# A memset on GpSimd between consecutive indirect DMAs, in a linear-attention and mixture-of-experts kernel

## What is computed

```python
q, k, v, gate = x @ Wq.T, x @ Wk.T, x @ Wv.T, x @ Wg.T     # 16 heads of 8
beta  = sigmoid(x @ Wb.T)
alpha = exp(-exp(A_log) * softplus(x @ Wa.T + dt_bias))
for t in range(512):                                        # the delta rule
    S = S * alpha_t
    delta = (v_t - k_t @ S) * beta_t
    S = S + outer(k_t, delta)
    y_t = q_t @ S
x = layernorm(x + (rmsnorm(y) * norm_w * silu(gate)) @ Wo.T + bo)
e = argmax(x @ router_w.T)                                  # one of 8 experts per token
ye = (silu(x @ gate_w[e].T) * (x @ up_w[e].T)) @ down_w[e].T    # inner size 352
out = layernorm(x + ye)
```

## Time and profile before

| | us |
|---|---|
| median of 3 runs | 781.5 |
| lowest, highest | 775.88, 783.81 |
| profiled execution, its own time | 779.52 |
| span of its profile | 777.7 |
| TensorE busy | 677.5 |
| VectorE busy | 610.1 |
| GpSimd busy | 654.0 |
| ScalarE busy | 415.8 |

### The profile page before, as it was taken

The page is one execution under the profiler, slowest core; times in us unless marked ns, Lnnn a source line. Parts: engine busy times, 40 slices in busy tenths (PEclk is TensorE's granted clock), DMA queues, the critical chain, the costliest instruction groups (busy, mean ns, idle before and its releaser), DMA issues.

```text
span 777.7 us, 13705 instructions
## 1 busy us (share of the span) xinstructions
PE 677.5 (87%) x3545; PEld 507.4 (65%) x3545; DVE 610.1 (78%) x1554; ACT 415.8 (53%) x1281; POOL 654.0 (84%) x800
## 2 busy tenths in 40 slices
PE   8779798989989899999989989697788879999990
PEld 3446374756657575565756657575667879999990
DVE  3899999999999999999999999999953523333340
ACT  6735456564565656466565555433314346666660
POOL 2899899999999999999999999999755756766664
PEclk9889899999999999999999999799869999999995
DMA  6733233443333334333234232206346456777720
GB/s 175 198 97 98 69 98 86 114 116 90 86 90 94 89 112 116 96 85 102 82 105 120 77 97 71 85 22 220 136 164 184 166 182 226 240 237 235 238 97 9
DMA packets 135917, 97.27 MB, mean 125 GB/s; under 512 B 95630, under 2 KB 110225, under 8 KB 135714
## 3 DMA queue, kind: packets, MB, share of 16 engines
q1 hardware_dynamic: 130514, 87.55, 38.2%
q0 software_dynamic: 4320, 8.43, 3.4%
q10 hardware_dynamic: 1008, 0.43, 0.2%
HBM read 39.80 MB, written 31.43 MB: 92 GB/s over the span
## 4 chain that ended last, share of the span: by engine, by line
DVE 35%; PE 29%; POOL 20%; issue 5%; ACT 5%; DMA 3%; SPq 2%; POOLq 0%; DVEq 0%; ACTq 0%
PE banks L432 11%; DVE banks L1817 6%; DVE upd L1805 6%; POOL q_prod L1255 6%; PE banks L654 5%; PE banks L445 5%; DVE banks L1791 5%; DVE prod L1775 4%; DVE banks L1801 4%; DVE mix L1795 3%; POOL u L1255 3%; DVE upd L1786 3%; POOL solve L1255 2%; POOL kkqk L1255 2%; POOL u_tmp L1255 1%
## 5 line engine op out<-in xcount | busy, mean ns | idle before, releaser
L1255 POOL TENSOR_TENSOR q_prod<-s_keep,q_gam 128x512 f32<-128x512 f32 x128 | 139.9, 1097 | 12.0 <-ACT s_keep L965 11.7
L707 PE MATMUL banks<-q_prod,ident 128*128 128x256 f32 x496 | 118.9, 395 | 21.6 <-POOL q_prod L1255 21.4
L965 ACT ACTIVATE s_keep<-banks 128x128 f32<-128x128 f32 x128 | 49.8, 389 | 156.7 <-DVE upd L1805 156.6
L707 PEld LDWEIGHTS banks<-q_prod,ident 128*128 128x128 f32 x496 | 95.7, 198 | 46.2 <-POOL q_prod L1255 32.4
L542 DVE TENSOR_TENSOR hid<-banks,silu 128x384 f32<-128x384 f32 x71 | 39.6, 557 | 96.4 <-PE banks L432 83.8
L432 PE MATMUL banks<-xs_t,w_tile 128*128 128x128 f32 x852 | 108.9, 278 | 3.5 <-ACT silu L473 3.5
L1817 DVE TENSOR_REDUCE banks<-upd 128x128 f32<-128x640 f32 x127 | 105.0, 827 | 7.6 <-ACT z_s L1194 0.5
L432 PEld LDWEIGHTS banks<-xs_t,w_tile 128*128 128x128 f32 x852 | 102.4, 194 | 4.4 <-issue 4.3
L1791 DVE TENSOR_REDUCE banks<-prod 128x64 f32<-128x576 f32 x128 | 93.7, 732 | 0.0
L654 PE MATMUL banks<-kkqk,ident 128*128 128x320 f32 (+2 forms) x272 | 84.5, 471 | 7.7 <-ACT y_rms L993 4.3
L1775 DVE TENSOR_TENSOR prod<-banks,k_gam 128x512 f32<-128x512 f32 x128 | 88.1, 688 | 2.9
(11 more groups left out here) (214 smaller groups left out, 1442.3 us busy)
## 6 DMA issues: line engine op xcount, KB each, us to landing
w_tile<-gate_up_we SPq DMA_DIRECT2D x71, 352.0 KB, 3.0
xs<-x_sorted SPq DMA_DIRECT2D x71, 64.5 KB, 2.4
x_ct<-in_x_ct SPq DMA_DIRECT2D x16, 256.0 KB, 3.2
k_dram<-kq_s SPq DMA_DIRECT2D x16, 256.0 KB, 2.9
q_dram<-kq_s SPq DMA_DIRECT2D x16, 256.0 KB, 3.6
out<-v_s SPq DMA_DIRECT2D x16, 256.0 KB, 2.7
out<-beta SPq DMA_DIRECT2D x16, 256.0 KB, 2.6
k_h<-k_dram SPq DMA_DIRECT2D x16, 256.0 KB, 3.0
```

Source lines behind the costliest of these rows:

```text
L707: i = mm(out, ident[:, :], q_prod[m][:, :, d, :], start=(m == 0 and d == 0), stop=(d == DH - 1), skip_group_check=True)
L1255: b.step(label, win, lambda: tt(out, x, y, op))
```

## The change

GpSimd gets a buffer `pause` of 128x128 float32, which nothing reads, and a semaphore `s_pause`. In `to_sorted`, from group 24 on, it clears `pause` after each indirect DMA, and each next indirect DMA waits for that. In `scatter` it does the same after the tiles 0 to 66 of 71. The 40 memsets of `to_sorted` and the 67 of `scatter` count on one semaphore. Nothing is taken away. The buffer is allocated ahead of those of the expert stage that follow, which lie 512 bytes further on in each partition.

```diff
+        pause, s_pause = sb("pause", [P, 128]), sem("s_pause")
...
         def to_sorted(eng, t0, t1):

             for m in range(t0, t1):
+                if m > WA * TW:
+                    eng.wait_ge(s_pause, m - WA * TW)
                 eng.indirect_dma_start(t["x_sorted"], bass.IndirectOffsetOnAxis(ap=place[:, m:m + 1], axis=0),
                                        x1_all[:, m, :], None).then_inc(s_sorted_a if m < WA * TW else s_sorted, 16)
+                if m >= WA * TW:
+                    if m > WA * TW:
+                        eng.wait_ge(s_pause, m - WA * TW)
+                    nc.gpsimd.memset(pause[:, :], 0.0).then_inc(s_pause, 1)
...
             def scatter(tile):
                 after(eng, s_norm, tile)
+                eng.wait_ge(s_pause, NT - WA * TW + min(tile, NF - 4))
                 eng.indirect_dma_start(t["out"],
                                        bass.IndirectOffsetOnAxis(ap=xs[tile % NR][:, D:D + 1].bitcast(I32), axis=0),
                                        rows_out[tile % NO][:, :], None, bounds_check=past_end, oob_is_err=False) \
                     .then_inc(s_scat[tile % NO], 16)
+                if tile < NF - 4:
+                    nc.gpsimd.memset(pause[:, :], 0.0).then_inc(s_pause, 1)
```

## The result

The changed kernel takes 796.76 us (median of four runs, 795.28 to 797.96) against 781.23 of the kernel before (four runs beside it, 775.88 to 783.81): a ratio of 1.0207, 95% interval 1.0150 to 1.0264. It is about 2% slower; the interval reaches from 1.5% to 2.6%. The forecast was 783.1 within 776 to 788, no change. The medians are 15.5 us apart. The two profiled executions lie further apart: 797.96 us with a span of 796.2, which is 18.5 more than the span of 777.7 before.

What follows compares the result with a forecast made beforehand. Bounds: SyncE's weight loads at the changeover, TensorE in the expert stage, GpSimd alone at the end. Sort-out 0.2, ScalarE 0, expert stage 0, end 1.4 sum to 1.6 us; on the median 781.5 that gives 783.1, range 776 to 788.

Steps and rivals of the forecast that it cites:

- The memset, 0.20 us: Each added 128x128 memset on GpSimd: 0.20 us, by a straight line between traced 128x1 and 128x2048 memsets.
- The lower price of 0.11 us: GpSimd's memset if only its length counted: 0.11 us, making the six at the end 0.6 us cheaper.
- G: Cost of a pause between two indirect DMAs: their new distance less 1.26 us.
- G in the sort-out, 0.20: Pause between to_sorted's DMAs: 0.20 us taken, so 23 pauses make the last DMA 4.6 us later.
- G for the scatters, 0.23: Pause between scatter DMAs: 0.23 us taken, within 0.18 to 0.29; a memset ahead of an rstd adds 0.22.
- The slack of 4.4 us: Changeover to the second part: last sort-out DMA lands 4.4 us before SyncE's weight loads finish, leaving 0.2 us exposed.
- Expert stage, 0: 640 to 752 us: GpSimd falls behind 3.2 us in rounds of four scatters, hidden, caught up later; cost 0.
- The cover of 3.7 us: Expert stage: rstd ended at 683.85, its reader rows_out started at 687.55, so 3.7 us of GpSimd's backlog is hidden.
- The end, 1.4: After the rstd of 752.89: four pauses between scatters and two memsets before an rstd add 1.4 us, bounds 0.4 to 1.7.
- the pause is dear: Rival: memset costs 0.46 us, G 0.40 to 0.51, sort-out and end expose 10.3 us, giving 791.8; chance 0.10.
- The last test that the prediction named: Expert stage: the forecast is wrong if xs_t waits for ScalarE's rows_out in the rounds of four.
- its second test: Changeover to the second part: the forecast is wrong if TensorE restarts over 2 us later.

Runs made afterwards that it cites:

- e1: The changed kernel with all memsets, the waits for them moved from the indirect DMAs to the next memset: 781.41 us against 782.01 before, ratio 0.9983.
- e2: The changed kernel with the two waits ahead of a DMA swapped, the memset's written first: 782.26 us against 782.01 before, ratio 0.9992.
- e5: The kernel before with the change in scatter alone, none in to_sorted: 796.43 us, ratio 1.0183 against before.
- f7: The kernel before with 128x720 memsets in scatter only and no DMA waiting for them: 797.47 us against 781.37, ratio 1.0200.
- f3: The kernel before, without memsets, each scatter given a second wait (s_var) that is always met already: 780.46 us against 781.37, ratio 0.9999.
- f6: The changed kernel with memsets of 128x1 instead of 128x128, all waits kept: 787.88 us against 781.37 before, ratio 1.0077.
- e4: The kernel before with the change in to_sorted alone, scatters as before: 783.03 us, ratio 1.0014 against before.
- f0: The changed kernel once more, word for word: 798.15 us against 781.37 before, ratio 1.0219.
- g9: The kernel before with two weight loads instead of five ahead of SyncE's wait for x_sorted, plus to_sorted's pauses; slower chip: 799.14 us against 818.88, ratio 0.9765.
- k4: The kernel before with the change in to_sorted alone, on a slower chip: 805.62 us against 821.11, ratio 0.9841.
- k0: The changed kernel again, on a slower chip: 802.71 us against 821.11 before, ratio 0.9800.
- k1: The changed kernel with all memsets but no DMA waiting for one, on a slower chip: 819.58 us against 821.11 before, ratio 1.0001.
- e6: The changed kernel with memsets of 128x1, all waits kept, on a slower chip: 808.54 us against 821.73 before, ratio 0.9863.
- e3: The kernel before, without memsets, each scatter given a second, always met wait (s_var), on a slower chip: 822.52 us against 821.73, ratio 1.0014.
- k5: The kernel before with the change in scatter alone, on a slower chip: 817.46 us against 821.11, ratio 0.9965.

## Why the prediction was wrong, by its own steps

- **The memset, 0.20 us: right**, 0.22 to 0.23. The Trainium skill (Perfetto Trace Analysis, GPSIMD Engine Instruction) advises against taking GpSimd's reported spans at face value. Here they add up: 0.96 + 0.22 + 0.28 = 1.46, the measured distance. The lower price of 0.11 us, which the prediction itself inferred beside that rule, did not come.
- **G in the sort-out, 0.20: right for a DMA with one wait**, 1.46 - 1.26. The prediction's seams were the measured ones: 0.17 without a wait (e1) and 0.28 with the own semaphore, a difference of 0.11, its very allowance from the earlier trace rows. It missed the second size. Five of the DMAs of the last block are the first of a call and wait for `place` too, 0.50 more each. From the first to the last DMA of the block it is 636.79 - 600.60 = 36.19 us, before 627.68 - 598.55 = 29.13: 7.1 more = 23 x 0.20 + 5 x 0.50.
- **G for the scatters, 0.23: the step that failed.** It is 0.70 (1.98 - 1.28). The prediction bounded it at 0.29 by rows in which a wait for GpSimd's own result comes alone, and wrote that a wait for the memset is added without counting what the scatter waits for already. `scatter` has `after(eng, s_norm, tile)` on the line above. e2 against the change shows that the order of the two waits alone, in `scatter` and in `to_sorted`, is worth 14.5 us, 796.76 against 782.26. Nearly all of it is the scatters' (e5, 796.43).
- **The slack of 4.4 us: right.** The last DMA landed 3.07 us after its start, as the earlier trace rows had it. From the `rstd` of window 15 to TensorE's restart it is 40.58 to 41.19 us where the sort-out is that of before (before, e5, f7, f3), 41.00 with the last block 2.0 us longer (e1), 40.83 and 41.58 with 4.5 (f6, e2), and 42.19, 42.68 and 43.10 with 7.1 (e4, the change, f0). SyncE's weight loads come last at the changeover in e1 and e2; in f6, e4, the change and f0 it is the landing of the last DMA. So the edge lies near 4.5 us. Of 7.1 us 2.7 would be exposed; measured are 1.6 to 2.5, in part because the `xs` load took 1.93 us instead of 2.38 in the change. Predicted were 0.2, for 4.6 us: the slack held, and the five second waits were missing.
- **Expert stage, 0: wrong by the failed term and by nothing else.** The formula of the step stands: with G = 0.70 a round of four gets 3 x 0.70 + 0.22 = 2.32 more, 0.38 were to spare, so six rounds fall behind by 11.6; measured 11.3. The cover of 3.7 us stands too, and ScalarE's idle time behind it took up a further 1.9. (The prediction's 0.96 us of idle time per tile is too high: by the earlier trace rows it is (112.00 - 73.99) / 52.8 tiles = 0.72. Nothing else hangs on it.) But the prediction's rounds of three had 1.67 - 0.68 = 1.0 us to catch up with. Now 2 x 0.70 + 0.22 = 1.62 of the 1.67 are gone (6.25 against 6.36 us), the backlog is carried through eleven rounds to the end, and from 7.5 us on TensorE waits for it.
- **The end, 1.4: the count right, the price not.** With G = 0.70 four pauses and two memsets are 4 x 0.70 + 2 x 0.22 = 3.2; measured 3.2. In e1, at 0.09, it was 15.14 - 14.48 = 0.7.
- **The rival "the pause is dear"** pointed the right way and not at the cause. It named 791.8 us and more, put the edge at G = 0.42, said that the rounds of four run away beyond it, and had 10% of the chance. It looked for the price in the memset's length, 0.46 us; the price is in the wait, and with a memset of 0.13 us the seam is 0.78 still (f6).
- **The last test that the prediction named** was the right one: DMAs over 1.6 us apart and `xs_t` late in the rounds of four. TensorE's restart over 2 us later, its second test, came too (4.2, of which 2.1 are the sort-out). In the changed profile the first hole of TensorE is ahead of a matmul of gate and up:

```profile
684.56 1.60 PE L439 MATMUL banks<-xs_t,w_tile 128*128 128x128 f32 x12 [1.61 <-ACT xs_t L469]
```

None of the experiments on chips of the first kind beats the kernel before: e1 and e2 equal it. On the slower chips g9, the earlier rows with the pauses in the sort-out, has the best ratio (0.9765; the change alone 0.9800 on another such chip). Whether the earlier rows alone gain on a chip of the first kind was not tried.

## What to carry to other kernels

Before adding a wait to an instruction, count the waits that it has: in front of an indirect DMA of GpSimd the wait that is met last belongs first, and a second one met late costs 0.50 us each time. An engine that is "not the bottleneck" has a budget per round, and it is the round with most spare time that decides whether a backlog is a passing one (e2) or is carried to the end (the change). And a change of about 2% should be timed on more than one chip, since here its sign differed between two kinds of them.

## What was not expected of the hardware

- **Two waits on an indirect DMA.** Met late, the first-written wait costs a seam of 0.28 us after a memset; the second-written one appears as a piece of its own on the sequencer (0.02 us) and the DMA starts 0.73 us after that. Already met, it costs nothing (f3: 1.28 apart).
- **Seams behind a GpSimd memset.** 0.17 us to a DMA without a wait, -0.05 to an `rstd`; the memset takes 0.13 us for 1 column, 0.23 for 128 and 0.73 for 720. A gap of 0.30 before a DMA behind a DMA is partly filled by a memset: 0.24 us of work costs 0.09.
- **Two kinds of chip.** The same kernel takes 781 to 782 us on some chips and 819 to 822 on others. The busy times of e3 and of the kernel before agree within 0.5% up to 550 us; what differs comes with the indirect DMAs that GpSimd issues close together, when the other engines wait for something that the trace doesn't name. DMAs 1.46 and 1.96 us apart instead of 1.35 gave back 9.8 us (k4) to 11.6 (k0) of k1's 53.2 between the two `rstd`; 1.35 and 1.85 (e6) gave back 1.7, no more than 1.26 (e3, 51.8).
- **The scatters there.** Scatters 1.98 us apart cost nothing on these chips (k5 0.9965), since the stage of 122.55 us takes 138.76 there without pauses and 136.41 with them. 1.87 apart it takes 129.57 (e6).
